# x*Wx0 of an LSTM by 7 block products for 8 steps, carried by DMA to the rows of the seeds, with the state's slices taken by input half

## What is computed

```python
xW = jnp.einsum('ntd,dk->tnk', x, Wx) + b          # layer 0: (512, 16, 2048)
def step(carry, xw_t):
    prev_h, prev_c = carry
    a = xw_t + prev_h @ Wh
    i, f, o = sigmoid(a[:, :H]), sigmoid(a[:, H:2*H]), sigmoid(a[:, 2*H:3*H])
    g = tanh(a[:, 3*H:])
    next_c = f * prev_c + i * g
    next_h = o * tanh(next_c)
    return (next_h, next_c), next_h
...
x = x + layer0(x)                                   # y0
h = tanh(h @ Wh1 + (x @ Wx1 + b1))                  # layer 1, step by step
x = x + layer1(x)                                   # y1, the output
```

## Time and profile before

| | us |
|---|---|
| median of 3 runs (2289.81 to 2290.33) | 2289.94 |
| the profiled execution | 2287.48 |
| its span in the trace | 2285.6 |
| TensorE busy | 2242.9 (98%) |
| VectorE busy | 1974.7 (86%) |
| ScalarE busy | 1642.1 (72%) |
| GpSimd busy | 1.8 |

### The profile page before, as it was taken

One profiled execution on the slowest core, in us unless ns is written; L12 is line 12 of the kernel. 1 busy time (PEld: TensorE's weight loads), 2 busy tenths in 40 slices (PEclk: granted clock), 3 DMA queues, 4 the chain that ended last, 5 costly groups with the idle time before them and its releaser, 6 DMA issues.

```text
span 2285.6 us, 150617 instructions
## 1 busy us (share of the span) xinstructions
PE 2242.9 (98%) x65564; PEld 1617.4 (71%) x65564; DVE 1974.7 (86%) x10283; ACT 1642.1 (72%) x5662; POOL 1.8 (0%) x10
## 2 busy tenths in 40 slices
PE   5999999999999999999999999999999999999997
PEld 2677777777777777777777777777777777777775
DVE  6888888888888888888888888888888888888887
ACT  5777777777777777777777777777777777777775
POOL 0000000000000000000000000000000000000000
PEclk9999999999999999999999999999999999999999
DMA  5000000000000000000000000000000000000000
GB/s 209 9 23 18 23 18 23 13 18 23 23 18 20 16 18 23 22 19 13 18 23 23 18 23 13 18 23 23 18 13 18 23 23 18 23 14 18 23 13 13
DMA packets 16738, 54.03 MB, mean 24 GB/s; under 512 B 2256, under 2 KB 2384, under 8 KB 14800
## 3 DMA queue, kind: packets, MB, share of 16 engines
q1 hardware_dynamic: 16080, 44.41, 5.5%
HBM read 27.62 MB, written 16.78 MB: 19 GB/s over the span
## 4 chain that ended last, share of the span: by engine, by line
PE 97%; DVE 2%; ACT 1%; issue 1%; POOL 0%; DVEq 0%; ACTq 0%; POOLq 0%
PE rec_ps L178 39%; PE in_ps L178 38%; PE rnn_ps L178 20%; ACT wh_part L478 1%; DVE largest_slice L277 0%; DVE turned L353 0%; DVE wh_part L321 0%; DVE uv L365 0%; DVE h_parts L381 0%; DVE pre_sb L359 0%; ACT gates_cell L502 0%; DVE h_parts L389 0%; ACT wx_sb L466 0%; DVE turned L403 0%; ACT rnn_ps L498 0%
## 5 line engine op out<-in xcount | busy, mean ns | idle before, releaser
L178 PE MATMUL in_ps<-wx_sb,x_sb 128*32 128x512 f32 x8192 | 977.4, 594 | 22.4 <-ACT wx_sb L466 22.4
L178 PE MATMUL rec_ps<-wh_part,h_parts 128*32 128x256 f16 x32704 | 988.9, 273 | 4.4 <-DVE h_parts L389 4.4
L178 PEld LDWEIGHTS rec_ps<-wh_part,h_parts 128*32 128x32 f16 x32704 | 867.5, 97 | 12.1 <-issue 7.0
L353 DVE STREAM_TRANSPOSE turned<-rec_ps 128x256 f32<-128x256 f32 x1024 | 460.4, 450 | 201.2 <-PE rec_ps L178 155.7
L178 PEld LDWEIGHTS in_ps<-wx_sb,x_sb 128*32 128x32 f32 x8192 | 258.9, 110 | 332.1 <-issue 318.9
L178 PEld LDWEIGHTS rnn_ps<-wx_sb,y 128*32 128x32 f32 x8192 | 247.0, 110 | 302.6 <-issue 301.1
L488 ACT ACTIVATE rec_ps<-in_ps,mask_scaled 128x256 f32<-128x256 f32 x1022 | 405.8, 434 | 2.0 <-PE in_ps L178 1.6
L178 PE MATMUL rnn_ps<-wh_part,h_parts 128*32 128x128 f16 x16352 | 323.4, 219 | 7.9 <-DVE h_parts L417 7.9
L178 PE MATMUL rnn_ps<-wx_sb,y 128*32 128x128 f32 x8192 | 318.4, 273 | 1.3 <-ACT rnn_ps L498 1.3
L502 ACT ACTIVATE gates_cell<-gate_ps,unscale 128x128 f32<-128x128 f32 x511 | 187.5, 367 | 181.2 <-DVE gate_ps L359 181.2
L498 ACT ACTIVATE rnn_ps<-rnn_ps,mask_scaled 128x128 f32<-128x128 f32 x511 | 174.8, 342 | 188.4 <-DVE turned L403 188.1
(11 more groups left out here) (52 smaller groups left out, 1272.9 us busy)
## 6 DMA issues: line engine op xcount, KB each, us to landing
x_sb<-xT SPq DMA_DIRECT2D x32, 512.0 KB, 3.7
yT<-y SPq DMA_DIRECT2D x64, 256.0 KB, 2.0
wh_sb<-wh SPq DMA_DIRECT2D x5, 1024.0 KB, 9.6
wx_sb<-wx SPq DMA_DIRECT2D x5, 1024.0 KB, 18.1
b_sb<-b SPq DMA_DIRECT2D x1, 256.0 KB, 2.7
b_sb<-b SPq DMA_DIRECT2D x1, 64.0 KB, 12.2
h_first<-h0T SPq DMA_DIRECT2D x1, 32.0 KB, 19.9
```

What stands on the lines that cost most here:

```text
L178: last = nc.tensor.matmul(out[QUAD * q:QUAD * (q + 1)], states, weights(q), start=False, stop=True, tile_position=(0, QUAD * q), skip_grou ...
L353: nc.vector.transpose(turned0[:, half].rearrange("p b n -> p (b n)"), rec0_ps[t % 2][half][:, 0:COLSH]).then_inc(turned0_done[half], 1)
```

## The change

**x*Wx0** is computed by groups of 8 steps. A group's 8 steps are two runs of 4 (a1, a2), its 512 features two halves, and Wx0 has four blocks of 256 x 1024. A 2 x 2 product of blocks needs 8 block products; here 7 are made from sums of blocks: GpSimd forms four sums of x per group (sum_x) and, once, three sums of weights and one in place (sum_wx0). A block product has 64 stationary columns (4 steps x 16), two slices and two column tiles of 64 side by side; its 128 rows are 2 tiles. The first group is made by 4 plain products of 4 slices.

ScalarE copies a finished product from PSUM to one of four stages in SBUF, scaled (copy_product), and puts the bias into the bank for two products in seven. SP moves each stage by two DMAs of 128 KB to the rows of seeds_sb that it belongs to, 16 partitions each, after the seeds that stood there have been read. A product goes to the low or the high group of 16 rows of its tile, so that VectorE's add of the two groups, made anyway, sums two products of a result; the other additions accumulate in PSUM. The seed of a step is then one copy of 512 columns from SBUF, without a mask. A product is cut into four pieces (a slice, 256 columns), and pieces_until(t) says how many have to be done after step t: 8 in each of the first two steps, 6 in steps 2 to 6, 5 in step 7 and then 3 and 4 by turns. Two pieces of one slice go as one matmul of 512 columns where they fall in one step.

**The recurrent product** takes the slices by input half: slices 0 and 1 for both gate halves, then, after h0_ready of state half 1, slices 2 and 3 for both.

**y0 and y1** are computed on GpSimd, y0 by two operations (h0_true, y0), with new waits: VectorE's state_full on h0_unscaled of the step before, ScalarE's tanh of layer 1 on y1_done of the step before. On VectorE the high part of state half 0 stands ahead of the cell of half 1. input1's four slices of a pair are split 3 and 1 between the two steps instead of 2 and 2. x is loaded by groups of 8 steps in four slots. Layer 1's weights are searched and scaled ahead of the loop; the first state is scaled too.

```diff
...
+def pieces_until(t):
+
+    ramp = 2 * FIRST_PIECES + FIRST_PIECES * (t + 1) if t < 2 else FIRST_PIECES * FIRST_PRODUCTS + 6 * (t - 1)
+    return min(ramp, LEAD + PIECES * PRODUCTS * (t + 1) // GROUP, ALL_PIECES)
...
+            def move(m):
+
+                g, i = group_of(m)
+                run, n_half, low = PLACE_OF[g > 0][i]
+                sp.wait_ge(copied, m + 1)
+                if g:
+                    sp.wait_ge(seed0_done, GROUP * (g - 1) + RUN * (run + 1))
+                for r in range(TILES):
+                    row = QUAD * (TILES * n_half + r) + BATCH * low
+                    sp.dma_start(seeds_sb[row:row + BATCH, RUN * run:RUN * (run + 1), :],
+                                 stage_sb[m % STAGES][TILE * r:TILE * (r + 1), :]).then_inc(moved[m % STAGES], 16)
...
+                out, one, op, other = ((sums[:, 0], a21, ALU.add, a22), (sums[:, 1], sums[:, 0], ALU.subtract, a11),
+                                       (sums[:, 2], a11, ALU.subtract, a21), (sums[:, 3], a12, ALU.subtract, sums[:, 1]))[i]
+                nc.gpsimd.tensor_tensor(out, one, other, op).then_inc(x_summed, 1)
...
+            for t in range(END):
+                s = t - LAG
+                if s >= 1:
+                    add_y1(s - 1)
+                if t < STEPS:
+                    add_y0(t)
+                if 1 <= t < 5:
+                    late_sum_wx0(t - 1)
+                g, i = divmod(t + 14, GROUP)
+                if g >= 2 and g < GROUPS and i < 4:
+                    sum_x(g, i)
...
+            def piece(m, k, lo, hi):
+
+                states, weights = product(m)
+                start = start_of(m) == NO_BIAS and k == 0
+                for r in range(TILES):
+                    last = nc.tensor.matmul(prod_ps[m % 2][TILE * r:TILE * (r + 1), lo:hi], states(k), weights(k, r)[:, lo:hi],
+                                            start=start, stop=True, tile_position=(0, TILE * r), skip_group_check=True)
+                return last
...
-                for half in range(HALVES):
-                    cols = slice(half * COLSH, (half + 1) * COLSH)
-                    for k in range(SUB):
-                        if t and half == 0 and k % SUBH == 0:
-                            pe.wait_ge(h0_ready[k // SUBH], t)
-                        for part in weights:
-                            last = tiles(rec0_ps[t % 2][half][:, 0:COLSH], states[:, k], lambda q: part[:, k, q, cols])
-                    last.then_inc(rec0_done[half], 1)
...
+                for k_half in range(HALVES):
+                    if t:
+                        pe.wait_ge(h0_ready[k_half], t)
+                    for half in range(HALVES):
+                        cols = slice(half * COLSH, (half + 1) * COLSH)
+                        for k in range(SUBH * k_half, SUBH * (k_half + 1)):
+                            for part in weights:
+                                last = tiles(rec0_ps[t % 2][:, 512 * half:512 * half + COLSH], states[:, k],
+                                             lambda q: part[:, k, q, cols])
+                        if k_half == HALVES - 1:
+                            last.then_inc(rec0_done[half], 1)
...
-                    p, half = divmod(t + 3, PAIR)
-                    if p < PAIRS:
-                        input0(p, half)
+                if t < STEPS:
+                    pieces(pieces_until(t - 1) if t else 2 * FIRST_PIECES, pieces_until(t))
...
                     gate_products(1, n)
+                    state_high(0, n)
                     cell(1, n)
-                    state_high(0, n)
-                if rnn_state:
-                    add_y1(s - 1)
-                if lstm:
+                    state_full(0, n)
                     state_low(0, n)
                     state_high(1, n)
+                    state_full(1, n)
                     state_low(1, n)
...
+            def copy_product(m):
+
+                act.wait_ge(prod_done, m + 1)
+                if m >= STAGES:
+                    act.wait_ge(moved[m % STAGES], moved_count(m - STAGES))
+                nc.scalar.activation(stage_sb[m % STAGES][:, :], prod_ps[m % 2][:, 0:COLS], ACT.Copy,
+                                     scale=hw_scale[:, :]).then_inc(copied, 1)
+                if m + 2 < ALL_PRODUCTS and start_of(m + 2) in (BIAS_FIRST, BIAS_SECOND):
+                    act.wait_ge(copied, m + 1)
+                    bias_product(m + 2)
...
-                for half in range(HALVES):
-                    last = nc.scalar.activation(rec0_ps[t % 2][half][:, 0:COLSH], in0_ps[t // PAIR % 2][:, half * COLSH:(half + 1) * COLSH],
-                                                ACT.Copy, scale=own)
-                last.then_inc(seed0_done, 1)
+                nc.scalar.activation(rec0_ps[t % 2][:, :].rearrange("p (h c) -> p h c", h=HALVES)[:, :, 0:COLSH],
+                                     seeds_sb[:, c].rearrange("p (h c) -> p h c", h=HALVES), ACT.Copy).then_inc(seed0_done, 1)
...
```

435 lines of the change are left out of this document (298 added, 137 removed).

## The result

| | us |
|---|---|
| before, median of 4 runs (2289.81 to 2291.28) | 2290.14 |
| changed, median of 4 runs (2415.92 to 2427.61) | 2422.03 |
| ratio, 95% interval | 1.0582 (1.0569 to 1.0594) |
| forecast | 2321 (2270 to 2395) |
| profiled execution of the changed kernel | 2427.61 |

The direction was right. The size was not: +132 us in place of +31, above the range's upper end. Of all runs one, the first of e3, was slow (9899 us, at a granted clock of 1.0 in its records); it is left out of e3's median.

The account below looks back on a forecast made before the run. TensorE was taken to set the pace at 4.345 us a step, with 0.09 us of room before the recurrence loop. The new loop of 4.405 adds 0.06 us over some 503 steps, +30 us: 2321 us, range 2270 to 2395.

Parts of the forecast that it names:

- Moves hidden, 2 to 4 us: DMA and SP: 14 moves of 128 KB per 8 steps take 2 to 4 us each, hidden, issued some 7 us early.
- seeds late: Rival: moves take 12 us instead of 4 from queue contention, each run of four steps waits some 5 us: +600; chance 0.02.
- The new loop, 4.405: Recurrence loop per step: 1.11 + 0.435 + 2.71 + 0.15 = 4.405 us, above the old 4.25 and TensorE's 4.15.
- 1.545 to transpose 0: Recurrent product's start to VectorE's transpose of gate half 0: 1.545 us instead of 1.11, since half 0 completes after 48 matmuls.
- transpose 1 at once after the add: VectorE's chain: transpose 1 follows 0.21 after the first add instead of 0.39, saving 0.18 us.
- The term of 2.71: VectorE's chain from transpose 0 to the end of h_parts' low half 0: 2.71 us in place of 2.99.
- TensorE's own step, 4.125 to 4.17: TensorE's work per step: recurrent product 1.74 + products 1.505 + layer 1 0.88 = 4.125 us, say 4.13 to 4.17.
- wide tiles: Rival: 64-wide tiles don't fill the array; with blocks at twice 1.505 the step is 5.63, time near 2937; chance 0.03.
- 0.2 to 0.3 us of waiting: Sign: TensorE's recurrent product waits for h_parts' low half 0 in every step, 0.2 to 0.3 us.
- GpSimd hidden: GpSimd's three to four operations a step take 0.5 to 2.1 us of 4.4, so they cost nothing.
- the rival of the shared port at 0.22: Rival: GpSimd and VectorE block each other, 0.05 to 0.15 us a step, 25 to 75 us, centre 2361; chance 0.22.
- start and end at 0 give or take 8: Start wins about 5 us by earlier weight search, loses 4 to 5 in the first seven steps: sum zero, give or take 8.

Follow-up runs that it names:

- e3: Changed kernel with y0 and y1 back on VectorE, GpSimd keeping only the sums: 2446.65 us, ratio 1.0703; once more for its trace, 2453.86 us.
- e2: Changed kernel with each move of seeds cut from 16 rows to one, leaving out 15/16 of the seeds: 2366.97 us, ratio 1.0348.
- e9: Changed kernel with each move cut from 512 columns to 32, as many packets but a sixteenth of the bytes: 2366.72 us, ratio 1.0339.
- e12: Changed kernel with a second buffer of seeds, so a product's two moves go once it is copied, nothing left out: 2369.33 us, ratio 1.0355.
- e1: Changed kernel with the recurrent product's old slice order restored (all slices for gate half 0 first): 2393.64 us, ratio 1.0453.
- e4: Changed kernel with GpSimd's sums of weights and first x put after the second search for the largest weight: 2423.05 us, ratio 1.0588.
- e7: Changed kernel with each block product on four 32-wide tiles instead of 64-wide ones, twice the matmuls: 2482.44 us, ratio 1.0846.
- e8: Changed kernel with 32-wide product tiles, old slice order, and VectorE's cell 1 ahead of high part 0 again: 2419.70 us, ratio 1.0576.
- e10: Kernel before, plus 14 unread moves of 128 KB per 8 steps, two in each of seven steps: 2300.65 us, ratio 1.0049.
- e13: Changed kernel with two seed buffers, 32-wide product tiles, and old order of slices and of VectorE's cell and high part: 2324.72 us, ratio 1.0171.
- e15: Kernel before, plus 14 unread moves of 128 KB per 8 steps, in bursts of 6 and 8: 2344.30 us, ratio 1.0241.
- e5: Kernel before with only the new slice order by input half in the recurrent product: 2367.04 us, ratio 1.0342.
- e11: Changed kernel with 32-wide product tiles, old slice and cell order, moves cut to one row of 16: 2265.44 us, ratio 0.9895.
- e16: Changed kernel with two seed buffers, 32-wide tiles, old slice and cell order, a product's second move held until VectorE's first add: 2272.03 us, ratio 0.9933.

## Why the forecast missed, point by point

**Moves hidden, 2 to 4 us: they cost 55 us. This is the step that failed most.** The forecast's paragraph on DMA and SP put the 14 moves at nothing, because their data are early and what is queued behind them on SP has time. They land in 4.5 us, and but for one step at the start nobody waits for their data. Yet their bytes, falling together, stop TensorE within its products: 58 us of long steps in the profiled execution, and 55 us less in the time when the bytes go (e2, e9) or are spread out (e12). I weighed when the seeds are due, but did not ask what else uses the DMA engines, nor, from the code, that the wait for the seeds' place bunches the moves. The rival "seeds late" held for a single step: 5.33 us ahead of ScalarE's seed at 93.16.

In nine traces (after, e1, e3's single run, e4, e7, e8, e10, e13, e15) TensorE's matmuls and weight loads both stand idle for over 0.5 us, later than 150 us into the run and ended by "issue", 318 times. All 318 stops end 1.2 to 2.0 us after such a packet has landed; the packets come every 4.2 to 4.6 us, so some 60 would do so by chance. The stop shown above ends at 1306.23; its packet started at 1302.92 and landed at 1304.68, with the DMA engines full meanwhile. Before, e2, e5, e9, e11, e12 and e16 have no such stop. The packets took 1.04 us at the median before, and 2 of 476 took over 1.6; in after 1.25, and 128 of 428 over 1.6. Not each late packet makes a stop, and in after the steps with a stop of over 0.3 us carry 44 of the 60 us above the median step; the others are spread over smaller delays. By which way the full engines make a packet late, no run here shows.

The Trainium skill, SBUF — State Buffer, "Who interferes with whom", says that DMA never contends with a compute engine. For the SBUF's ports no run here speaks against that, but as a rule for the time it does not hold: e15 changes nothing but transfers and loses 55 us.

**The new loop, 4.405: it measured 4.47.** The mechanism, 1.545 to transpose 0 and transpose 1 at once after the add, was right, and e5 confirms its price by itself. The term of 2.71 was 0.07 short, and that is worth some 30 us over the run. Tanh of half 0 came when forecast (1.86 after transpose 0), and so did uv of half 1. Mis-sized was the handing over from ScalarE to VectorE. The forecast took 0.04 from a row in which both operations are VectorE's (2267.36 to 2267.40 in the earlier trace rows). From the end of a tanh to the high part that waits for it it is 0.10 at the median of all 392 steps, for half 0 and half 1 alike (1209.88 to 1209.98 above, 1209.22 to 1209.33 for half 0).

**TensorE's own step, 4.125 to 4.17: it measured 4.43.** This term was mis-sized too. I kept the 0.86 of a block and asked whether wide tiles fill the array (they do: 0.43 a piece) but not what it costs to go to them and back. That is 0.12 + 0.15 a step (e1 against e7 and e8), and more than the whole saving of 0.215. The rival "wide tiles" was looking for a loss in proportion to the columns; the loss is a fixed one per visit. In the changed kernel itself it costs next to nothing, since the loop of 4.46 lies just above 4.43: it is why TensorE does not show the 0.2 to 0.3 us of waiting that was forecast, and why undoing the order in e1 gave 0.04 us a step and not 0.16.

**GpSimd hidden; the rival of the shared port at 0.22.** In the even step the rival came to almost nothing: between 400 and 2200 us 376 of 392 first adds take their 0.30 us, and the other 16, each beside y1, 0.02 to 0.17 more, 1 us in all. The copy took 0.67 (0.64 forecast), y 0.33 to 0.37 (0.15 to 0.52). But the start had the same lock at its worst, 9.3 us, and I had put start and end at 0 give or take 8. The start alone came to 20.8.

**The start and the clock.** The forecast's own reading was off here: the product at 65.04 in the earlier trace rows is not number 4 but number 5 (the products before it start at 44.50, 49.18, 53.42 and 59.08). So before stood 3.2 us above an even pace there (20.54 - 4 x 4.345), not 7.5, and of the 5 us that the start was to win there at most 3.2 could be had. Of the 20.8 us 8.9 lie ahead of recurrent product 1 (53.35 against 44.50 in the earlier trace rows), and e4 shows 7 of them to be the lock. The other 12.0 lie in the seven steps after it (98.91 - 53.35 against 78.08 - 44.50): 5.3 in the last, 9.61 us long, in which the seeds were late (in e2, with small moves, it takes 4.85), and 2.9 in the first. TensorE had stood for 7.58 us when recurrent product 1 began, and the granted clock in the 7 us from 51 was 0.51, the lower level, where before it was 1.00; this product took 3.60 us to its end, 1.94 in the earlier trace rows.

```profile
53.35 3.60 PE L373 MATMUL rec_ps<-wh_part,h_parts 128*32 128x256 f16 x64 [7.58 <-DVE h_parts L642]
```

**The sum.** Even steps 59 us (30 forecast), stops 58 (0), start 20.8 (0): together 138 of the 140 us; the last 2 lie behind the last recurrent product (20.9 against 18.3 us to the end). The forecast had 30 of them. The direction came from the loop, which was worked out; the loop and TensorE's own step hid each other's room, and this the forecast did not see.

**What stays open.** How the stops of 60 us in e13 follow from pairs of moves, when the same pairs cost after nothing (e12) and before 13 us. Its 25 stops over 0.5 us are of the same kind, and e16 removes them, so they too come from bytes falling together; why this variant is more sensitive no run shows.

## What to carry to other kernels

A count of columns is not the time of TensorE if the tiles' width changes between neighbours: look for the fixed price of each visit, and keep one width where the groups are short. Transfers whose data are early can still cost time by falling together; ask of every wait in front of a DMA whether it bunches those behind it, and give them a second buffer and a pace before giving them up. And when one engine's room is worth 0.1 us a step, size its new step from rows at the seams (from group to group, and from engine to engine), not from the groups alone.
